# Gated cross-attention and experts on one core: the opening of the first layer rearranged

## What is computed

```
x = x + tanh(g_xattn[l]) * attention(layernorm(x), context, context, mask, Wq..Wo, bq..bo)
x = x + tanh(g_ffn[l])   * experts(layernorm(x))

attention: q, k, v = x Wq + bq, c Wk + bk, c Wv + bv, in 16 heads of 16
           softmax(q k / 4 + mask * -1e9) v, then Wo and + bo   (mask in layer 0 only)
experts:   each token goes to 2 of 8 experts by router logits;
           layer 0: silu(x Wg) * (x Wu), then Wd (hidden 688); layer 1: relu(x W1)^2 W2
```

## Time and profile before

| | us |
|---|---|
| median of three runs | 766.17 |
| lowest and highest of them | 762.58 and 766.7 |
| the profiled execution, its time | 769.0 |
| the profiled execution, span from first to last instruction | 767.3 |
| mean granted TensorE clock in it, share of full speed | 0.952 |

### The profile page before, as it was taken

One profiled execution on the slowest core, in us unless ns is written; L12 is line 12 of the kernel. 1 busy time (PEld: TensorE's weight loads), 2 busy tenths in 40 slices (PEclk: granted clock), 3 DMA queues, 4 the chain that ended last, 5 costly groups with the idle time before them and its releaser, 6 DMA issues.

```text
span 767.3 us, 17444 instructions
## 1 busy us (share of the span) xinstructions
PE 678.0 (88%) x5804; PEld 520.4 (68%) x5804; DVE 415.0 (54%) x1385; ACT 274.4 (36%) x528; POOL 214.4 (28%) x399
## 2 busy tenths in 40 slices
PE   5798999859999999999999999978888885999970
PEld 3666767637777777777777777657666663788850
DVE  4777888753333333233332332469989876454426
ACT  3556576411211112112111112256555541354530
POOL 4122553460111111111111011212355436344440
PEclk9999999859999999999999999999999986899995
DMA  9044554461131131111011010320112122544428
GB/s 218 18 144 138 182 179 141 148 220 43 56 101 51 36 79 35 35 32 39 28 35 36 29 28 21 143 92 29 58 64 70 64 85 78 151 125 121 123 83 328
DMA packets 50856, 70.71 MB, mean 92 GB/s; under 512 B 7687, under 2 KB 38023, under 8 KB 50771
## 3 DMA queue, kind: packets, MB, share of 16 engines
q1 hardware_dynamic: 42380, 50.85, 22.1%
q0 software_dynamic: 6816, 18.69, 6.9%
q10 hardware_dynamic: 1575, 0.05, 0.1%
HBM read 46.55 MB, written 23.02 MB: 91 GB/s over the span
## 4 chain that ended last, share of the span: by engine, by line
PE 69%; DVE 18%; issue 5%; DMA 4%; POOL 2%; ACT 2%; DVEq 0%; SPq 0%; POOLq 0%; ACTq 0%
PE ps L1482 28%; PE ps L1512 17%; PE ps L1299 4%; DVE m_rows L841 4%; PE ps L1495 3%; DVE x_sb L825 3%; PE ps L1312 2%; PE ps L1237 2%; DVE ctx_q L858 2%; PE ps L1468 2%; PE ps L1291 2%; DMA ys_dram<-share,dest_i 2%; PE ps L1265 2%; PE ps L1254 1%; DVE x_sb L875 1%
## 5 line engine op out<-in xcount | busy, mean ns | idle before, releaser
L1482 PE MATMUL ps<-w_all,share 128*128 x780 | 232.4, 446 | 4.2 <-DVE share L1118 4.2
L1482 PEld LDWEIGHTS ps<-w_all,share 128*128 128x128 f32 x780 | 146.9, 193 | 66.5 <-issue 8.4
L551 POOL DMA_INDIRECT ys_dram<-share,dest_i x78 | 75.9, 974 | 333.2 <-DVE share L1129 279.8
L1512 PE MATMUL ps<-w_all,share 112*128 (+1 forms) x624 | 147.9, 380 | 1.7 <-ACT share L737 1.0
L1512 PEld LDWEIGHTS ps<-w_all,share 112*128 112x128 f32 (+1 forms) x624 | 112.4, 190 | 15.1 <-issue 2.6
L1145 DVE TENSOR_TENSOR share<-share,ps 128x344 f32<-128x344 f32 x78 | 40.0, 513 | 140.5 <-PE ps L1482 79.3
L726 ACT COPY share<-ps 128x512 f32<-128x512 f32 x39 | 22.9, 587 | 151.9 <-PE ps L1495 151.9
L841 DVE TENSOR_REDUCE m_rows<-ps 128x8 f32<-128x960 f32 x64 | 70.4, 1139 | 11.0 <-PE ps L1254 10.9
L723 ACT ACTIVATE share<-ps 128x344 f32<-128x344 f32 x78 | 35.9, 460 | 106.9 <-PE ps L1482 106.9
L544 POOL DMA_INDIRECT xs_dram<-xn,slot_now x64 | 63.7, 996 | 21.9 <-issue 14.6
L514 POOL TENSOR_SCALAR nm<-mv 128x1 f32<-128x1 f32 (+1 forms) x48 | 12.4, 257 | 162.7 <-DVE mv L881 116.8
(11 more groups left out here) (202 smaller groups left out, 991.3 us busy)
## 6 DMA issues: line engine op xcount, KB each, us to landing
share<-xs_dram SPq DMA_DIRECT2D x78, 129.0 KB, 2.1
w_all<-ys_dram SPq DMA_DIRECT2D x16, 512.0 KB, 7.2
w_all<-gate SPq DMA_DIRECT2D x8, 688.0 KB
w_all<-up SPq DMA_DIRECT2D x8, 688.0 KB
w_all<-down SPq DMA_DIRECT2D x8, 560.0 KB
w_all<-w SPq DMA_DIRECT2D x16, 256.0 KB
xs_dram<-q_flat SPq DMA_DIRECT2D x17, 129.0 KB, 2.4
out<-x_sb SPq DMA_DIRECT2D x8, 256.0 KB, 5.6
```

The source lines that it names most:

```text
L551: g.indirect_dma_start(ys_dram, bass.IndirectOffsetOnAxis(ap=dest_i[:, u:u + 1], axis=0), y_sb[:, u, :], None).then_inc(D_y[u], 16)
L1482: i = t.matmul(ps[:, bank, 0:w], xgT[:, k, :], w_all[:, bass.ds(off + (k * UPW[l] + col - EW[l]), w)], start=(k == 0), stop=(k == KT - 1))
L1512: i = t.matmul(ps[:, 6, 0:D], hT[0:r, c + KD[1] * (j % 2) * l, :], w_all[0:r, bass.ds(off + (KT * UPW[l] + c * D - EW[l]), D)], start=(c = ...
```

## The change

- SP starts the context of batches 0 to 3 ahead of the tokens of batch 0.
- ACT gets one activation of a single column (`first_act`) behind its transfers, waiting for the identity matrix; the function table is loaded there. `ctx_evac(0)` now stands ahead of `ln1_apply` of batch 0.
- PE gets six float32 matmuls of 512 columns of the identity matrix with itself, into PSUM bank 7, ahead of `ctx_t(0)`. Nothing reads them.
- `split_mask` works by piece: batches 0 and 1 (240 columns) where the whole was, batches 2 and 3 (240) in unit 1, batches 4 to 7 (480) in unit 3, each ahead of `divide`. `scores` of units 4 and 8 wait for the pieces.
- `split_bias(0)` goes from ahead of `row_max(0)` into unit 0, ahead of `divide(0)`. PE's waits for Wo and for it go from ahead of unit 0 to ahead of the first `out_proj`.
- The mask's working rows lie in expert slot 5 of `w_all` in place of `share`, since `share` is in use by unit 1. Slot 5 is loaded only when output projection 11 is done.

```diff
--- before.py
+++ after.py
@@ -134,8 +134,9 @@
 
         yg = w_all[:, NE * EW[1]:NE * EW[1] + NB * QT * TOPK * D].rearrange("p (b t k d) -> p b t k d", b=NB, t=QT, k=TOPK)
 
-        mask_f = share[:, 0:NB * K].rearrange("p (b k) -> p b k", b=NB)
-        mask_hi = share[:, NB * K:NB * K + NB * K // 2].bitcast(BF16).rearrange("p (b k) -> p b k", b=NB)
+        mask_at = (NE - 3) * EW[0]
+        mask_f = w_all[:, mask_at:mask_at + NB * K].rearrange("p (b k) -> p b k", b=NB)
+        mask_hi = w_all[:, mask_at + NB * K:mask_at + NB * K + NB * K // 2].bitcast(BF16).rearrange("p (b k) -> p b k", b=NB)
         ctx_q = sb("ctx_q", [P, 2 * (2 * P + DH)])
         recT = sb("recT", [P, 2, 8])
         st1 = sb("st1", [P, 2, QT, 6])
@@ -193,6 +194,7 @@
         wcomb = sb("wcomb", [P, NT, TOPK])
 
         ident = sb("ident", [P, P])
+        first_act = sb("first_act", [P, 1])
         hmask = sb("hmask", [P, HP])
         emask = sb("emask", [P, 2])
         sel = sb("sel", [P, 4])
@@ -360,8 +362,8 @@
                 sp.dma_start(ctx_sb[0:K, 4 * h:4 * h + 4, :],
                              ctx_rows[4 * h:4 * h + 4, :, :].rearrange("b k d -> k b d")).then_inc(L_ctx[h], 16)
 
+            load_ctx(0)
             sp.dma_start(x_sb[:, 0:2, :], xv[:, 0:2, :]).then_inc(L_x[0], 16)
-            load_ctx(0)
             load_att(0, 1, L_wk)
             load_att(0, 0, L_wq)
             load_att(0, 2, L_wv)
@@ -594,6 +596,8 @@
             for g in range(4):
                 a.dma_start(mask_f[Q4 * g:Q4 * g + 3, :, :], mask.unsqueeze(0).to_broadcast([3, NB, K])).then_inc(L_mask, 16)
             a.dma_start(mask_col[0:K, :], mask.rearrange("b k -> k b"), allow_slow_non_contiguous=True).then_inc(L_mcol, 16)
+            a.wait_ge(C_id, 2)
+            a.activation(first_act[:, :], ident[:, 0:1], ACT.Identity, scale=ident[:, 0:1])
             for l in range(2):
                 def ctx_evac(h):
                     for k in range(KT):
@@ -665,8 +669,8 @@
                 B0, G0 = NB * l, NU * l
                 a.wait_ge(*((L_qk, 32) if l == 0 else (L_small1, 48)))
                 if l == 0:
+                    ctx_evac(0)
                     ln1_apply(B0)
-                    ctx_evac(0)
                     k_evac(0, 0)
                     k_evac(0, 1)
                     xnT_evac(B0, 2)
@@ -773,20 +777,23 @@
                 v.tensor_tensor(bq4[:, l, :, :], bq[:, l, :].unsqueeze(2).to_broadcast([P, KT, 2]),
                                 qs[:, :].unsqueeze(1).to_broadcast([P, KT, 2]), ALU.mult).then_inc(C_q, 1)
 
-            def split_mask():
-
-
-                v.wait_ge(L_mask, 64)
-                v.wait_ge(C_e, 3)
-                v.tensor_scalar(mask_f, mask_f, mk[:, 0:1], -NEG, ALU.mult, ALU.mult).then_inc(d_m, 1)
-                v.wait_ge(d_m, 1)
+            def split_mask(piece):
+
+
+                a, z = ((0, 2), (2, 4), (4, NB))[piece]
+                part_f, part_hi, at_ = mask_f[:, a:z, :], mask_hi[:, a:z, :], 6 * piece
+                if piece == 0:
+                    v.wait_ge(L_mask, 64)
+                    v.wait_ge(C_e, 3)
+                v.tensor_scalar(part_f, part_f, mk[:, 0:1], -NEG, ALU.mult, ALU.mult).then_inc(d_m, 1)
+                v.wait_ge(d_m, at_ + 1)
                 for part in range(1, 3):
-                    v.tensor_copy(mask_hi, mask_f).then_inc(d_m, 1)
-                    v.wait_ge(d_m, 2 * part)
-                    v.scalar_tensor_tensor(out=mask_f, in0=mask_hi, scalar=mk[:, 1:2] if part == 1 else sel[:, 2:3], in1=mask_f,
+                    v.tensor_copy(part_hi, part_f).then_inc(d_m, 1)
+                    v.wait_ge(d_m, at_ + 2 * part)
+                    v.scalar_tensor_tensor(out=part_f, in0=part_hi, scalar=mk[:, 1:2] if part == 1 else sel[:, 2:3], in1=part_f,
                                            op0=ALU.mult, op1=ALU.add).then_inc(d_m, 1)
-                    v.wait_ge(d_m, 2 * part + 1)
-                v.tensor_copy(mask3[:, :, :], mask_f).then_inc(d_m, 1)
+                    v.wait_ge(d_m, at_ + 2 * part + 1)
+                v.tensor_copy(mask3[:, a:z, :], part_f).then_inc(d_m, 1)
 
             def split_bias(l):
 
@@ -934,13 +941,11 @@
                     ln1_stats(B0)
                     first_consts()
                     query_bias(0)
-                    split_mask()
+                    split_mask(0)
                     v.wait_ge(L_mcol, 16)
                     v.tensor_scalar(mask_col[0:K, :], mask_col[0:K, :], NEG, None, ALU.mult).then_inc(C_v, 2)
                     ln1_stats(B0 + 1)
                     values(B0, 6)
-                    v.wait_ge(C_a, 1)
-                    split_bias(0)
                 else:
                     query_bias(1)
                     v.wait_ge(L_b1, 32)
@@ -984,6 +989,11 @@
                         ln1_stats(B + 2)
                     if even and b >= 2:
                         route1(B - 2)
+                    if l == 0 and u == 0:
+                        v.wait_ge(C_a, 1)
+                        split_bias(0)
+                    if l == 0 and u in (1, 3):
+                        split_mask(1 + u // 2)
                     divide(G)
                     if l == 0 and u in FILL_V:
                         values(B0 + FILL_V[u], 5)
@@ -1331,6 +1341,10 @@
 
                 B0, G0 = NB * l, NU * l
                 if l == 0:
+
+                    for _ in range(6):
+                        t.matmul(ps[:, 7, :].rearrange("p (j n) -> p j n", j=4), ident[:, :],
+                                 ident[:, :].unsqueeze(1).to_broadcast([P, 4, P]), start=True, stop=True)
                     ctx_t(0)
                     t.wait_ge(L_wk, 16)
                     k_proj(0, 0)
@@ -1383,8 +1397,6 @@
                 if l == 0:
                     t.wait_ge(C_sel, 2)
                 max_t(G0)
-                t.wait_ge(L_wo, 32 * (l + 1))
-                t.wait_ge(C_bo, l + 1)
                 t.wait_ge(*((L_vr, 32) if l == 0 else (L_small1, 48)))
 
                 for u in range(NU):
@@ -1400,6 +1412,8 @@
                         t.wait_ge(a_xnT, min(B + 2, B0 + NB))
                         if even and b >= 3:
                             t.wait_ge(d_rk, B - 2)
+                        if l == 0 and u in (3, 7):
+                            t.wait_ge(d_m, 6 * (2 + u // 7))
                         scores(G + 1)
 
                     if u >= 1:
@@ -1420,6 +1434,9 @@
                         t.wait_ge(d_max[0], G + 2)
                     if u >= 3:
                         route(G - 3, 1)
+                    if u == 1:
+                        t.wait_ge(L_wo, 32 * (l + 1))
+                        t.wait_ge(C_bo, l + 1)
                     if u >= 1:
                         out_proj(G - 1)
                     if u + 1 < NU:
```

## The result

The changed kernel took 762.51 us in the median of 12 runs (756.85 to 769.17), the kernel before 766.43 in 12 runs beside it (759.92 to 768.13); ratio 0.994, interval 0.9912 to 0.9967. The change was repeated twice later: medians 765.55 and 763.76, inside the range, with ratios 1.0002 (0.9974 to 1.0031) and 0.997 (0.9938 to 1.0002), whose intervals reach or pass 1.

What follows compares the result with a forecast made beforehand. PE was taken to set the pace from unit 0, DVE close behind, after an opening of engine handovers. Opening gain 1.5 us against losses of 0.14, 1.68 and 0.15 gave +0.4: 766.6 us, range 762.8 to 769.2.

Steps and rivals of the forecast that it cites:

- The opening on ACT and PE: Opening: identity matmuls 7.3 us, key projection 3.4 in place of 5.47, queries start 15.3 in place of 16.98, gain 1.7.
- What is late next: Opening, ACT: tanh still waits for `bo` until 17.27, so `q_evac` follows and the first scores gain 0.7 us, not 1.7.
- the far end: Opening: upper end of the first scores' gain, 1.7 us, if the transfers land 1 us earlier.
- rival 1: Pieces hidden and bias landing a microsecond earlier: 763.7; only one of the two, 765.0 or 765.6; chance 0.25 with halves.
- The bias ahead of the maxima: Unit 0, DVE: without the bias split ahead, `row_max(0)` starts 0.06 behind the scores; gain 0.86 us, context copy costing 0 to 0.1.
- the two waits moved out of PE's way: PE's waits for Wo and the bias, moved to ahead of the first `out_proj`: cost nothing, no gain counted.
- The bias in unit 0: Unit 0, DVE: six bias instructions take 2.38 us against 2.24 idle ahead of `divide(0)`; loss 0.14 us.
- The pieces: Mask pieces on DVE: unit 1's makes PE stand still 1.68 us more ahead of `shifted(2)`; unit 3's costs 0.15 us.
- The sum: Whole change: -1.5 + 0.14 + 1.68 + 0.15 = +0.4 us, giving 766.6.
- that 0.05 in the chances: Chance 0.05 for a shift of the clock's course at the end of the attention stage.
- Rivals 2 and 3: 2: PE slow through all identity matmuls, 771.3, chance 0.05. 3: speed falls back before key projection, 767.7, within a shared 0.15.

Runs made afterwards that it cites:

- pieces_only: Kernel before with the mask split in pieces and PE's waits for Wo and the bias moved; units 1 to 5 scores 34.65 us apart against 33.15.
- before_again: The kernel before, unaltered, run again for a second profile and its spread; 765.87 us, ratio to its own kernel 1.001.
- after_x_first: The changed kernel with the tokens of batch 0 loaded ahead of the context again; 762.54 us, run once.

## Why the prediction was wrong

**The opening on ACT and PE: right up to the tanh.** Identity matmuls 7.35 us (forecast 7.3), key projection 3.46 (3.4), queries at 15.40 (15.3), in the first profile. In the other two the identity matmuls took 7.97 and 7.55 us, since the speed rose later, and the queries came at 16.03 and 15.61.

**"What is late next": the step that failed.** It put the tanh at 17.27, from one profile of the kernel before, and allowed a gain of 0.7 us for the first scores. The tanh ran at 16.19, 16.30 and 16.16 in three profiles of the changed kernel, and `q_evac` behind it waited for the queries, not for `bo`. It started at 16.61, 17.23 and 16.81, where the forecast had 17.48. The first scores gained 1.58, not 0.7, in the first profile; over the three profiles of each kernel (20.37, 19.89 and 20.52 against 18.79, 19.41 and 18.99) they gained 1.2 in the mean.

The prediction counted 8.7 us from the issue of `bo` and said that nothing ahead of that transfer shrinks. The time to landing was 8.8 us again, but the issue came 1.16 us earlier. SP's issues in the first profile of the kernel before, then of the changed kernel:

```profile
3.96 2.13 SPq L370 DMA_DIRECT2D x_sb<-x  x1
...
8.52 0.59 SPq L373 DMA_DIRECT2D bo<-bo  x1
```

```profile
4.37 0.56 SPq L372 DMA_DIRECT2D x_sb<-x  x1
...
7.36 0.59 SPq L375 DMA_DIRECT2D bo<-bo  x1
```

SP spent 2.13 us on issuing the tokens of batch 1 in the profile that the forecast was read from, and 0.43 to 0.79 in all sixteen others; no other profile issued `bo` as late as 8.52. Issue and time to landing together put `bo` at 16.3 to 17.2 in the seven profiles with ACT's old order and at 16.0 to 17.0 in the ten with the new one. The 17.27 was the latest of all. So most of this miss is one slow opening taken for the usual one; whether the change itself brings `bo` earlier, and why that issue took 2.13 us, is open. The prediction named 1.7 as the far end, and the half of rival 1 in which only `bo` comes early gave 765.6, which is the picture of the traces.

**The bias ahead of the maxima: right.** 0.98 for 0.86. The term itself came to 0.77: 0.86 less the 0.1 that the forecast allowed behind it. The other 0.21 is the two waits moved out of PE's way, which the forecast put at nothing (0.61 to 0.40 ahead of unit 1's scores, also in pieces_only). **The bias in unit 0:** 0.02 for 0.14.

**The pieces: mechanism right, size a little off.** 1.48 us of pause for 1.68 in unit 1, since six instructions on 240 columns took 2.20 and not 2.31; nothing for 0.15 in unit 3. In all 1.5 for 1.97 (bias included). The estimate by the page "VectorE: DVE Perf Modes" of the Trainium skill, 1.4 us for a piece, is off the other way; the measured rows of DVE stand nearer.

**The sum.** Forecast +0.4 at the scores of unit 5; measured -1.07 in the first pair and -0.9 in the mean of three profiles each. In the first pair the terms are 0.88 for the first scores, 0.12 for the bias and the waits ahead of unit 1, 0.12 for the bias in unit 0 and 0.35 for the pieces, together the 1.47 between forecast and trace. The pieces give back 1.5 of some 2.4 us, which was the forecast's picture, with the opening's half too small.

**The rest of the measured 3.9 us is not the change's opening.** A gain of about 1 us carried through would give 765.4 from the 766.43 beside it, inside the range. The range's lower end allowed 0.9 us below rival 1 for the spread; the medians of three sets of the same changed kernel were 762.51, 765.55 and 763.76. So the first set fell below the range by chance, and that the other two lie inside it is no merit of the forecast, whose gain of the opening was too small against the mean of the profiles. The spread goes with TensorE's granted clock, and I had given that 0.05 in the chances. Rivals 2 and 3 did not come: the speed rose while the identity matmuls ran, and the key projection kept it through the transposes.

## What to carry to other kernels

Before moving work to make room, see whether it was in the way: the mask split took 5.3 us of DVE in which nothing on the path waited for it, and in pieces it came ahead of the one instruction that PE waited for. Two edits that each gain a microsecond in an opening may be the same microsecond; undo each by itself before counting both. And where TensorE idles ahead of a dense stage, look at the granted clock of the stage's first microseconds: a few matmuls without use in the idle time were worth as much here as the rearranged opening. And before a term is taken from one profile, compare it with a second one of the same kernel.

## What the runs showed of the hardware

- The granted clock column reads 1.00 from the start of an execution although TensorE begins at its lower level. The first matmuls of the kernel before were 0.80 us apart for 480 columns and later ones 0.40; eight records of 512 columns took 6.42 to 6.50 us in the kernels with four identity matmuls, twelve 7.33 to 8.31 in those with six. Only the spacing shows it.
- 1.7 us between the end of the last identity matmul (8.95) and the key projection (10.63), filled with transposes and a wait, did not bring the lower level back (3.46 us for its eight records).
- The lower level also came in mid-kernel in some executions of a program and not in others. In before_again PE's 1.62 us of idle time ahead of `max_t(0)` was followed by a stretch at 0.58 from 27 to 31 us, in the first profile of the kernel before 1.38 us at the same place were not. In after_x_first 1.72 us of idle time were followed by 0.50 from 44 to 46 us, in five other profiles they were not.
